# Message-passing kernel: the encoder run for the source table first, four steps of gathers issued before the query table

## What is computed

```python
h = x @ enc_W + enc_b
for l in range(3):
    cat = concatenate([h[src], h[dst], edge_attr])
    m = relu(cat @ msg_W1[l] + msg_b1[l]) @ msg_W2[l] + msg_b2[l]
    agg = segment_sum(m, dst, num_segments=12500)
    h = gru_cell(agg, h, Wih[l], Whh[l], bih[l], bhh[l])
out = layernorm(x + relu(h @ ro_W1 + ro_b1) @ ro_W2 + ro_b2)
```

## Time and profile before

| what | us |
|---|---|
| median of three runs (6212.6 to 6212.83) | 6212.81 |
| the profiled execution: its own time | 6218.49 |
| its span, from the first to the last instruction | 6216.6 |
| POOL busy in the span | 4625.3 (74%) |
| DVE busy | 3524.2 (57%) |
| PE busy | 2874.1 (46%) |
| ACT busy | 345.5 (6%) |

### The profile page before, as it was taken

The page is one execution under the profiler, slowest core; times in us unless marked ns, Lnnn a source line. Parts: engine busy times, 40 slices in busy tenths (PEclk is TensorE's granted clock), DMA queues, the critical chain, the costliest instruction groups (busy, mean ns, idle before and its releaser), DMA issues.

```text
span 6216.6 us, 71434 instructions
## 1 busy us (share of the span) xinstructions
PE 2874.1 (46%) x6986; PEld 1569.7 (25%) x6986; DVE 3524.2 (57%) x4596; ACT 345.5 (6%) x542; POOL 4625.3 (74%) x4865
## 2 busy tenths in 40 slices
PE   4444444444444444444444444444444444444444
PEld 3222222222222222222222222222222222222222
DVE  5555555555555555555555555555555555555555
ACT  1000000000000000000000000000000000000001
POOL 6777777777777677777777777767777777777776
PEclk6666666666656655656555565556566565656656
DMA  4222222222222122222222222212222222222221
GB/s 127 50 49 49 49 49 49 49 49 49 49 49 49 40 48 48 48 48 48 47 48 48 48 48 48 48 44 47 48 48 47 46 49 45 48 48 48 48 48 36
DMA packets 350333, 307.50 MB, mean 49 GB/s; under 512 B 148483, under 2 KB 236553, under 8 KB 349463
## 3 DMA queue, kind: packets, MB, share of 16 engines
q0 software_dynamic: 155328, 159.81, 13.6%
q1 hardware_dynamic: 117167, 109.08, 6.1%
q10 hardware_dynamic: 77328, 33.96, 2.1%
HBM read 279.43 MB, written 22.83 MB: 49 GB/s over the span
## 4 chain that ended last, share of the span: by engine, by line
POOL 69%; issue 23%; SPq 3%; DVE 2%; DMA 2%; PE 1%; ACT 0%; DVEq 0%; ACTq 0%; POOLq 0%
POOL p_src L734 69%; SPq L441 2%; SPq L437 1%; DMA q_tab<-p_src 1%; DVE work_ps L1413 1%; DMA p_src<-p_tab,idx_all 0%; DMA p_src<-p_tab 0%; DVE p_src L1410 0%; PE bank L929 0%; PE bank L930 0%; DVE folds L1429 0%; PE bank L765 0%; DVE state L1448 0%; ACT p_src L994 0%; PE bank L885 0%
## 5 line engine op out<-in xcount | busy, mean ns | idle before, releaser
L734 POOL DMA_INDIRECT p_src<-p_tab,idx_all x4830 | 4599.4, 952 | 1559.0 <-issue 1471.1
L1410 DVE TENSOR_TENSOR p_src<-work_ps,p_src 128x512 f32<-128x512 f32 x624 | 431.2, 691 | 2495.6 <-DMA p_src<-p_tab,idx_all 2283.5
L885 PE MATMUL bank<-hot,folds 128*128 128x96 f32 x2496 | 657.1, 411 | 1855.2 <-DVE folds L1429 1787.9
L872 PE MATMUL work_ps<-w_edges,msg 128*128 128x512 f32 x1248 | 1115.9, 994 | 28.3 <-DMA windows_sb<-q_tab 28.3
L885 PEld LDWEIGHTS bank<-hot,folds 128*128 128x128 f32 x2496 | 528.3, 294 | 2124.6 <-DVE folds L1429 1996.6
L1424 DVE SCALAR_TENSOR_TENSOR work_ps<-work_ps,rel 128x1024 f32<-128x1024 f32 x624 | 768.5, 1232 | 21.5
L1413 DVE TENSOR_TENSOR work_ps<-p_src,bank 128x1024 f32<-128x1024 f32 x624 | 766.8, 1229 | 21.2
L1429 DVE TENSOR_REDUCE folds<-work_ps 128x256 f32<-128x1024 f32 x624 | 757.6, 1214 | 0.1
L882 PE MATMUL bank<-hot,counts 128*34 128x96 bf16 x416 | 66.9, 254 | 909.7 <-DVE folds L1429 909.7
L929 PE MATMUL bank<-state,gate_w 128*128 128x468 f32 x324 | 266.8, 923 | 454.5 <-ACT chunk_sum L1073 324.5
L872 PEld LDWEIGHTS work_ps<-w_edges,msg 128*128 128x128 f32 x1248 | 309.5, 303 | 29.6 <-issue 15.8
(11 more groups left out here) (157 smaller groups left out, 1428.1 us busy)
## 6 DMA issues: line engine op xcount, KB each, us to landing
p_src<-p_tab ACTq DMA_DIRECT2D x9792, 0.2 KB
p_src<-p_tab SPq DMA_DIRECT2D x9792, 0.2 KB
p_src<-p_tab,idx_all POOLq DMA_INDIRECT x4830
msg<-in_edge_k SPq DMA_DIRECT2D x156, 256.0 KB
pick<-rel_tab SPq DMA_DIRECT2D x312, 96.0 KB
windows_sb<-q_tab ACTq DMA_DIRECT2D x312, 24.0 KB
windows_sb<-q_tab SPq DMA_DIRECT2D x312, 24.0 KB
pick<-q_tab ACTq DMA_DIRECT2D x312, 24.0 KB
```

The costliest lines, as they stand in the source:

```text
L734: pool.indirect_dma_start(out=p_src[r][0:rows, t, :], out_offset=None, in_=p_tab[l][0:NODES, :], in_offset=bass.IndirectOffsetOnAxis(ap=id ...
L872: nc.tensor.matmul(edge_ps[k % 2], attrs[n % 2][:, s, :], w1_edges[:, l, :], start=True, stop=True)
L885: last = nc.tensor.matmul(fold_ps, folds[:, b, :], hot_all[n % 2][:, s * BLOCKS + b, 1:WINDOW + 1], start=(b == 0), stop=(b == BLOCKS - 1))
L1410: nc.vector.tensor_tensor(rows, edge_ps[k % 2], rows, ALU.add).then_inc(with_edge, 1)
```

## The change

- The encoder runs 28 units (`UNITS`) of half the width: units 0 to 13 multiply by the source half only and store `p_tab[0]`, units 14 to 27 do the same x with the destination half and store `q_tab[0]`. There are four stages and four banks in place of two pairs (`STAGES`).
- SP loads only the indices of the first four steps ahead of the encoder; `dst_steps` goes out after the store of unit 1, `dst_i` after unit 4's, `first_i` after unit 7's, the rest of the indices and `raw_nodes` after unit 14's. `dst_steps` lies in an unused part of `sums` now, and DVE clears that part later.
- POOL waits for the stores of `p_tab[0]` alone and issues the 31 gathers of steps 0 to 3 (`PRE` = 4, semaphores `ahead`), and only then reads the flags; the other steps follow once all is stored.
- The fused weights are made inside the loop: PE waits for all 16 weights ahead of unit 6 (`FUSED_AFTER`), ACT copies them after unit 6. The ranges go ahead of unit 20.

The diff, cut to its core (waits and index arithmetic that only follow from the new names are left out):

```diff
-RANGES_AFTER = 10
+RANGES_AFTER = 20
+UNITS = 2 * ENC_PAIRS
+STAGES = 4
+ENC_STORED = 16 * UNITS // STAGES
+FUSED_AFTER = 6
+PRE = 4
...
-            sp.dma_start(dst_steps, io["dst_steps"]).then_inc(steps_in, 16)
-            sp.dma_start(dst_i[:], io["dst"]).then_inc(dst_in, 16)
-            sp.dma_start(first_i, io["dst_first"]).then_inc(first_in, 16)
-            sp.dma_start(idx_all[:], io["src"]).then_inc(idx_all_in, 16)
-            sp.dma_start(raw_nodes, io["src_single"]).then_inc(nodes_raw, 16)
-
-            for i in range(ENC_PAIRS):
+            sp.dma_start(idx_all[:, 0:PRE, :], io["src"][:, 0:PRE, :]).then_inc(idx_first_in, 16)
+
+            for u in range(UNITS):
+                i, s = u % ENC_PAIRS, u % STAGES
                 halves = 2 if i + ENC_PAIRS < CHUNKS else 1
-                sp.wait_ge(enc_staged, i + 1)
+                table = p_tab[0] if u < ENC_PAIRS else q_tab[0][0:NPAD, :]
+                sp.wait_ge(enc_staged, u + 1)
                 settle(sp)
-                for t, table in enumerate((p_tab[0], q_tab[0][0:NPAD, :])):
-                    sp.dma_start(enc_rows(table, i), enc_stage[i % 2][:, 0:halves, t].rearrange("p h j f -> p h (j f)")).then_inc(stored[i % 2], 16)
+                sp.dma_start(enc_rows(table, i), enc_stage[s][:, 0:halves].rearrange("p h j f -> p h (j f)")).then_inc(stored[s], 16)
+                if u == 1:
+                    sp.dma_start(dst_steps, io["dst_steps"]).then_inc(steps_in, 16)
+                if u == 4:
+                    sp.dma_start(dst_i[:], io["dst"]).then_inc(dst_in, 16)
+                if u == 7:
+                    sp.dma_start(first_i, io["dst_first"]).then_inc(first_in, 16)
+                if u == ENC_PAIRS:
+                    sp.dma_start(idx_all[:, PRE:, :], io["src"][:, PRE:, :]).then_inc(idx_all_in, 16)
+                    sp.dma_start(raw_nodes, io["src_single"]).then_inc(nodes_raw, 16)
...
+            pool.wait_ge(idx_first_in, 16)
+            for s in range(STAGES):
+                pool.wait_ge(stored[s], 16 * len(range(s, ENC_PAIRS, STAGES)))
+            for m in range(PRE):
+                for t in range(gathers_of(m)):
+                    pool.indirect_dma_start(
+                        out=p_src[m][:, t, :], out_offset=None, in_=p_tab[0][0:NODES, :],
+                        in_offset=bass.IndirectOffsetOnAxis(ap=idx_all[:, m, t:t + 1], axis=0)).then_inc(ahead[m], 16)
             passes, slow = load_flags(pool)
...
-                    for m in range(STEPS):
+                    for m in range(0 if l else PRE, STEPS):
...
+                if u == FUSED_AFTER:
+                    pe.wait_ge(weights_in, 16 * WEIGHTS)
+                    for l in range(LAYERS):
+                        nc.tensor.matmul(fused_ps[l][:, 0:3 * HID], w2t_b2[:, l, 0:2 * HID], wih[:, l, :], start=True, stop=True)
+                        nc.tensor.matmul(fused_ps[l][0:HID + 1, 4 * HID:7 * HID], w2t_b2[:, l, 2 * HID:], wih[:, l, :], start=True, stop=True).then_inc(vw_ps, 1)
...
-                if i >= 2:
-                    pe.wait_ge(enc_staged, i - 1)
+                if u >= STAGES:
+                    pe.wait_ge(enc_staged, u - STAGES + 1)
                 xv = x_halves[:, cols(i)].rearrange("q (p j) -> q j p", j=4)
                 for j in range(4):
-                    at = j % 2 * 4 * HID
-                    last = nc.tensor.matmul(enc_ps_of[i % 2][j // 2][0:CPART, at:at + 4 * HID], xv[:, j, :],
-                                            enc_w1[:].rearrange("q h n -> q (h n)"), start=True, stop=True)
+                    last = nc.tensor.matmul(enc_ps_of[u % STAGES][0:CPART, j * PAIR:(j + 1) * PAIR], xv[:, j, :],
+                                            enc_w1[:, :, t * HID:(t + 1) * HID], start=True, stop=True)
                 last.then_inc(enc_projected, 1)
...
-            for i in range(ENC_PAIRS):
-                act.wait_ge(enc_projected, i + 1)
-                if i >= 2:
-                    act.wait_ge(stored[i % 2], 32 * (i // 2))
-                for b, ps in enumerate(enc_ps_of[i % 2]):
-                    last = nc.scalar.copy(enc_stage[i % 2][:, :, :, 2 * b:2 * b + 2, :].rearrange("p h t j f -> p j h t f"),
-                                          ps[0:CPART, :].rearrange("p (j h t f) -> p j h t f", j=2, h=2, t=2))
-                last.then_inc(enc_staged, 1)
+            for u in range(UNITS):
+                act.wait_ge(enc_projected, u + 1)
+                if u >= STAGES:
+                    act.wait_ge(stored[u % STAGES], 16 * (u // STAGES))
+                nc.scalar.copy(enc_stage[u % STAGES].rearrange("p h j f -> p j h f"),
+                               enc_ps_of[u % STAGES][0:CPART, :].rearrange("p (j h f) -> p j h f", j=4, h=2)).then_inc(enc_staged, 1)
+                if u == FUSED_AFTER:
+                    act.wait_ge(setup, 1)
+                    for l in range(LAYERS):
+                        act.wait_ge(vw_ps, l + 1)
...
-            dve.wait_ge(enc_projected, ENC_PAIRS)
+            dve.wait_ge(enc_projected, UNITS)
...
-                dve.wait_ge(gathered[r], landed(k))
+                if k < PRE:
+                    dve.wait_ge(ahead[k], 16 * gathers_of(k))
+                else:
+                    dve.wait_ge(gathered[r], landed(k))
```

More of the change, by code:

```diff
@@ L159, in build @@
         p_src = [p_src_all[:, s] for s in range(GATHER_SLOTS)]
-        dst_steps = p_src_all[0:STEPS // 2, 0:4].rearrange("p s g f -> p (s g f)").bitcast(I32).rearrange("p (j e) -> p j e", j=2)
+        dst_steps = sums[0:STEPS // 2, ENC_PAIRS * CHUNK:ENC_PAIRS * CHUNK + 2 * STEP].bitcast(I32).rearrange("p (j e) -> p j e", j=2)
         hot_all = [sb(f"hot{s}", [128, GROUP * BLOCKS, HOT]) for s in range(2)]
@@ L198, in build @@
         stage = sb("stage", [CPART, 2, 4, HID])
-        enc_stage = [p_src_all[0:CPART, 4 + 2 * s:6 + 2 * s].rearrange("p a g f -> p (a g f)").rearrange(
-            "p (h t j f) -> p h t j f", h=2, t=2, j=4) for s in range(2)]
+        enc_stage = [p_src_all[0:CPART, 4 + s].rearrange("p g f -> p (g f)").rearrange("p (h j f) -> p h j f", h=2, j=4) for s in range(STAGES)]
         hid = sb("hid", [HID + 1, CHUNK])
@@ L282, in build @@
         enc_staged = sem("enc_staged")
-        stored = [sem(f"stored{s}") for s in range(2)]
+        stored = [sem(f"stored{s}") for s in range(STAGES)]
+        idx_first_in = sem("idx_first_in")
+        ahead = [sem(f"ahead{s}") for s in range(PRE)]
         idx_in = [sem(f"idx_in{h}") for h in range(2)]
@@ L351, in stored_before @@
         def stored_before(l, c):
-            return 32 * (c + CHUNKS * l + ENC_PAIRS // 2)
+            return 32 * (c + CHUNKS * l) + ENC_STORED
         def all_stored(eng, l, chunks=CHUNKS):
-            eng.wait_ge(stored[0], 32 * (chunks * l + ENC_PAIRS // 2))
+            eng.wait_ge(stored[0], 32 * chunks * l + ENC_STORED)
             if l == 0:
-                eng.wait_ge(stored[1], 32 * (ENC_PAIRS // 2))
+                for s in range(1, STAGES):
+                    eng.wait_ge(stored[s], ENC_STORED)
         def enc_rows(table, i):
@@ L506, in chunk_rows @@
             return rows[bass.ds(c, 1), 0:n].rearrange("o p j f -> (o p) j f")
-        enc_ps_of = [(sum_ps, zr_ps), (n_ps, pq_ps)]
+        enc_ps_of = [sum_ps, zr_ps, n_ps, pq_ps]
+        fused_ps = [work_ps[:, 512 * l:512 * (l + 1)] for l in range(LAYERS)]
         def pq_view(ps, n=CPART):
@@ L737, in _ @@
             with pool.Else():
+                for m in range(PRE):
+                    pool.wait_ge(ahead[m], 16 * gathers_of(m))
+                pool.wait_ge(idx_first_in, 16)
                 for l in range(LAYERS):
@@ L759, in _ @@
                     nc.tensor.matmul(apart_ps, units, apart[:], start=True, stop=True).then_inc(ranges_ps, 1)
[L760 to L761 removed]
+                if u >= STAGES:
+                    pe.wait_ge(enc_staged, u - STAGES + 1)
                 xv = x_halves[:, cols(i)].rearrange("q (p j) -> q j p", j=4)
                 for j in range(4):
[L764 to L766 removed]
+                    last = nc.tensor.matmul(enc_ps_of[u % STAGES][0:CPART, j * PAIR:(j + 1) * PAIR], xv[:, j, :],
+                                            enc_w1[:, :, t * HID:(t + 1) * HID], start=True, stop=True)
                 last.then_inc(enc_projected, 1)
[L769 to L776, removed]
+            pe.wait_ge(enc_staged, UNITS)
             pe.wait_ge(cleared, ONES)
@@ L987, in _ @@
             last.then_inc(w1_sb, 1)
-            for i in range(ENC_PAIRS):
-                act.wait_ge(enc_projected, i + 1)
-                if i >= 2:
-                    act.wait_ge(stored[i % 2], 32 * (i // 2))
-                for b, ps in enumerate(enc_ps_of[i % 2]):
-                    last = nc.scalar.copy(enc_stage[i % 2][:, :, :, 2 * b:2 * b + 2, :].rearrange("p h t j f -> p j h t f"),
-                                          ps[0:CPART, :].rearrange("p (j h t f) -> p j h t f", j=2, h=2, t=2))
-                last.then_inc(enc_staged, 1)
```

(11 more changed lines are left out.)

12 lines of the change are left out of this document (7 added, 5 removed).

## The result

| what | before | after |
|---|---|---|
| median, 8 runs each (us) | 6212.82 (6210.71 to 6216.31) | 6194.53 (6190.52 to 6195.37) |
| ratio, 95% interval | | 0.9968 (0.9957 to 0.9979) |
| span of the profiled execution | 6216.6 | 6192.8 |
| POOL's first gather | 64.56 | 41.95 |

A forecast was written before the change was run, and what follows sets the result against it. POOL's gathers were taken to bound the kernel, so an earlier start counts one for one: 17.5 us earlier less 1.4 for the flags is 16.1, span 6200.5, median 6196.7 us; 8-in-10 range 6190 to 6205.

The forecast's parts named there:

- What bounds the kernel: POOL's gathers: only its start at 64.56 us, gather count and layer turns move the end; the change touches the start.
- When the weights land: Last of 16 weights, awaited by PE ahead of unit 6, lands at 27.5 us, bounds 22 to 29.4.
- A unit's time: Units 7 to 13 on PE take 1.3 us each at full clock, bounds 1.04 to 2.07; 9.1 us together.
- PE rival: PE paces the table, 2.07 us a unit from slow clock or weight loads: first gather 54.4, time 6204.0; chance 0.13.
- The clock: After its stop PE runs fused products and unit 6 at half clock, 4.5 and 2.1 us, then full clock.
- The sum of the start: POOL's first gather at 47.1 us in place of 64.56, 17.5 us earlier; bounds 39.8 to 54.4.
- the tail from copy to gather: After unit 13: copy 0.6, issue 0.3, store landing 2.2, then 0.8 us to POOL's first gather.
- The price of the flags: POOL's read of the flags and branch behind gather 31 cost 1.4 us, between 0.3 and 2.8.
- What must be ready at gather 32: At 86.1 us the flags (by 56) and query table (landed by 67, at slowest 78) are ready.
- DVE's start and the ring: First sums stay at 85.6 us, give or take 5; seven slots leave POOL 33 us at step 10.
- The clears and the rule against the change: DVE and GpSimd lockout might slow the 31 gathers during DVE's clears; as rival 6.5 us lost, time 6203.2, chance 0.04.
- The median: Start gain 17.5 less 1.4 us for flags is 16.1 us off, giving 6196.7 us.

The follow-up runs named there:

- e2: Changed kernel with the loads of destinations, first destinations and all source indices issued ahead of the encoder again; single run, first gather at 50.33 us.
- e10: Changed kernel with the loads of destinations, first destinations and all source indices ahead of the encoder, on another chip; single run, span 6195.4 us.
- e4: Changed kernel with only 64 of 128 columns multiplied from unit 4 on; single run, first gather at 44.25 us.
- e3: Changed kernel with the fused weights made ahead of unit 14, not unit 6; ratio to the kernel before 1.0009 (0.9992 to 1.0025).
- e6: Changed kernel with seven more clears on DVE ahead of its first step; single run, span 6191.5 us.
- e7: Changed kernel with 18 more clears on DVE ahead of its first step; single run, span 6226.0 us.
- e5: Changed kernel with POOL's clear of 10.7 us done three times, not once, ahead of its wait for the source table; single run, span 6196.1 us.
- e12: The changed kernel itself, timed again beside the kernel before on another chip; median 6204.34 us against 6225.81, ratio 0.9964.
- e11: Changed kernel with the fused weights made ahead of unit 14, not unit 6, on another chip; median 6200.3 us, ratio to the kernel before 0.9959.
- e9: Changed kernel, but POOL waits for both tables and all source indices before its first gather; 6228.1 us against 6225.8 before, ratio 1.0003.

## Why the prediction was right, and where it was not

The forecast was 6196.7 us, faster by 16.1; measured 6194.53, by 18.3. What bounds the kernel and how the change acts on it was right. Two terms of the start were not, and point by point:

- **What bounds the kernel.** Right: all of the gain but 1.2 us of the profiled span stands before the first gather, and a layer takes what it took.
- **When the weights land.** Wrong, outside the bounds given: 20.34, not 27.5 (22 to 29.4). The step that failed was the claim that what lies beside the weights on SP's queue is "about the same". Over the whole start it was; but the stores and `dst_i` enter the queue only when the units they follow are staged, and by 20.3 us SP had issued only x, the indices of four steps, `dst_steps` and the first stores (`dst_i` went out at 21.24). The last weight took 8.57 us and not 17.6. e2 and e10 put the loads back, and the weights landed at 28.6 and 28.7.
- **A unit's time.** Mis-sized: 1.7 us, not 1.3. Units 7 to 13 took 11.8 us from 26.6 to 38.4, not 9.1. The argument from columns ("half of them at the full clock is 1.04") failed at this width: the time follows neither columns nor clock, as e4 and the windows beside it show. The part of the PE rival that spoke of narrow products paced by weight loads fits that, its price of 2.07 us does not: 2.07 is a unit that stands alone, with its start and its end (e3 has one at 73.97 us); in an unbroken run one follows the other every 1.7 us.
- **The clock.** Its level was foreseen, its price was not: PE, after 3.8 us without work, made the fused products and unit 6 at 0.50, in 4.1 and 2.1 us (4.5 and 2.1 predicted), and units 7 and 8 as well; from about 30 it was at the full clock. For the units that made no difference, 1.7 us at either level; the 2.1 of unit 6 is that of a unit with its start, not of its clock. The rows of the windows of the changed kernel, columns as in the earlier trace rows:

```profile
20.40:24.50 4.10, 4.10 (x12) 3.13 (x12) 0.00 (x0) 0.97 (x2) 4.10 (x1) 0.50 0.88 202
24.50:26.60 2.10, 2.10 (x11) 2.09 (x10) 1.34 (x1) 0.00 (x0) 2.10 (x1) 0.50 1.00 364
26.60:38.40 11.80, 11.80 (x57) 11.80 (x57) 11.28 (x12) 6.73 (x16) 0.25 (x1) 0.86 0.63 215
```

- **The sum of the start.** Weights -7.1, fused products -0.4, units +2.7, the tail from copy to gather -0.4: 41.95 in place of 47.1. Two errors of opposite sign; the bounds of 39.8 to 54.4 held, though the weights broke theirs.
- **The price of the flags.** 1.4 us predicted, 0 measured: gather 32 starts 0.30 us behind gather 31, as any gather does. POOL's sequencer read the flags at 65.7 and 66.8, while 12, then 11 of the 31 gathers were still to start. These are rows of the view of the tile `flags`:

```profile
L381 POOLq TENSOR_LOAD <-flags x1: 732/732/732, 65.7 to 65.7; - x1
L382 POOLq TENSOR_LOAD <-flags x1: 558/558/558, 66.8 to 66.8; - x1
```

- **What must be ready at gather 32.** Right. Unit 27 was copied at 63.3, and DVE had the flags at 53 (56 predicted).
- **DVE's start and the ring.** The start was right (86.4 for 85.6 "give or take 5"). The slack was right in kind, wrong in place: the tightest pair is step 7 on step 0 with 24 us, not step 10 on step 3 (e6, e7). By the prediction's own numbers it would have been 30 there, not 33. In the kernel before it was 46 us at step 7.
- **The clears and the rule against the change.** Right for the clears: gathers 18 to 23 lie beside the two clears of 2.79 us (64.02 and 67.44) and take 0.95 us each. What did hold up a gather was another form of DVE instruction, below.
- **The median.** 18.3 and 21.5 us on two chips, with 22.6 at the start. That is within the intervals. But the agreement of 16.1 and 18.3 is in part luck: the start gave 6.5 us more than the 16.1 forecast, and the median shows 2.2 of them. Why the first pair of medians differs by 4.3 less than the start is not shown.

## What to carry to other kernels

When one engine bounds the kernel from its first instruction to its last, find the first thing it really needs and run the preparation for that alone; everything else can lie under its first work, as far as the buffers let it run ahead. Before counting on that, find the earliest step that reuses a buffer: here its slack was the budget. Ask also for the condition: on the chip where single rows set the pace, the same head start was worth nothing. And a transfer lands late because of what is queued at the time, not of what is queued in total: move loads that nobody needs yet out of the queue rather than behind one another.

## What the runs showed of the hardware

**A DVE instruction with two SBUF inputs holds up a gather.** In the changed kernel one gather of the head start took 1.63 us in place of 0.95. It began just ahead of DVE's `rel_first` (two inputs in SBUF), and ended 0.78 us behind that one's end at 75.63:

```profile
74.78 1.63 POOL L720 DMA_INDIRECT p_src<-p_tab,idx_all  x1 [0.30 <-issue]
...
74.87 0.76 DVE L1532 TENSOR_TENSOR rel_first<-dst_i,base_all 128x416 f32<-128x416 int32 x1
```

```profile
5296.48 0.42 DVE L1505 TENSOR_TENSOR ysq<-yc 117x256 f32<-117x256 f32 x1
5296.57 1.15 POOL L756 DMA_INDIRECT p_src<-p_tab,idx_all  x1 [0.31 <-issue]
```

**Stretches move by themselves.** The wait at the turn to layer 1 was 27.9 to 28.4 us in five profiles (before, after, e5, e6, e12) and 23.2 to 25.9 in the five others (e7 to e11), with no order by when they started. And the median gather was 952 ns in most profiles, 955 in e2, e4, e11 and e12: over 4830 gathers 3 ns are 14.5 us. Kernels moved by about as much on one chip: the kernel before took 6213.2 in one run and 6222.6 to 6228.9 in the others, e9 6211.9 in the profiled run (952 ns) and 6225.6 to 6229.3 in the others; that it is the same thing isn't shown. It is why e9 and e12 are compared by their medians: their profiled executions, one with gathers of 952 ns and one of 955, are only 5.5 us apart in span. A single run of this kernel doesn't tell 5 us.
